# A decoder layer's last microseconds: three PSUM banks for the last down products, one residual moved, sixteen unread products added

## What is computed

```
x = x + q * scan(kv, sigmoid(a))            # gated linear recurrence over the 1024 rows
x = x + layernorm(softmax(q k^T) v Wout)    # 16 heads, 64 context rows and one null key
x = x + bitlinear(silu(bitlinear(n, w_gate)) * bitlinear(n, w_up), w_down)   # hidden width 1024
bitlinear(a, w): a rounded to 8-bit integers by its row's largest value, w rounded to -1, 0, 1
```

## Time and profile before

| what | value |
|---|---|
| median of 3 runs | 516.19 us (515.22 to 517.26) |
| the profiled execution's own time | 514.18 us |
| its span, from first to last instruction | 512.4 us |
| PE busy | 475.0 us, 93% |
| DVE busy | 421.3 us, 82% |
| ACT busy | 330.5 us, 65% |
| POOL busy | 303.9 us, 59% |
| mean granted TensorE clock | 0.992 |

### The profile page before, as it was taken

How to read it: one execution, slowest core, us unless ns; L and a number is a source line. 1 busy time by engine, 2 the same in 40 slices (tenths; PEclk the granted TensorE clock), 3 DMA queues, 4 the chain that set the end, 5 groups by cost and what they waited for, 6 DMA issues and landing times.

```text
span 512.4 us, 8915 instructions
## 1 busy us (share of the span) xinstructions
PE 475.0 (93%) x2962; PEld 389.2 (76%) x2962; DVE 421.3 (82%) x938; ACT 330.5 (65%) x456; POOL 303.9 (59%) x481
## 2 busy tenths in 40 slices
PE   1999999989988998999999999999999999999775
PEld 0777787867767887888888888888888888886433
DVE  5799998958427667899989899898998998987784
ACT  4545541345323434788888889788888888786651
POOL 2223224610001577798788797877878878888860
PEclk9999999999999999999999999999999999999996
DMA  8996000230000000011131211223232122121243
GB/s 262 324 353 252 2 1 1 56 68 0 1 1 1 0 3 6 6 27 42 36 58 37 53 36 43 53 52 38 47 47 47 43 38 56 42 48 42 62 105 91
DMA packets 67116, 31.80 MB, mean 62 GB/s; under 512 B 49664, under 2 KB 65280, under 8 KB 67072
## 3 DMA queue, kind: packets, MB, share of 16 engines
q1 hardware_dynamic: 67072, 31.24, 24.4%
HBM read 15.24 MB, written 4.19 MB: 38 GB/s over the span
## 4 chain that ended last, share of the span: by engine, by line
PE 67%; DVE 17%; POOL 4%; issue 4%; DMA 3%; SPq 3%; ACT 2%; DVEq 0%; POOLq 0%; ACTq 0%
PE psum L1252 34%; PE psum L1505 10%; PE psum L1510 9%; PE psum L1268 3%; DMA xs<-in_x_dram 3%; DVE region_a L940 2%; PE psum L1483 2%; PE psum L1491 2%; PE psum L1386 2%; SPq L394 2%; PE psum L1356 2%; PE psum L1373 1%; DVE region_d L1057 1%; DVE mx L1054 1%; DVE region_a L951 1%
## 5 line engine op out<-in xcount | busy, mean ns | idle before, releaser
L547 POOL TENSOR_TENSOR region_d<-region_d,rden 128x1024 f32<-128x1024 f32 x32 | 60.9, 1904 | 86.9 <-DVE rden L1071 86.9
L1252 PE MATMUL psum<-Mhi,xT2hi 128*128 128x260 f32 x256 | 75.0, 293 | 0.2
L1252 PE MATMUL psum<-Mlo,xT2hi 128*128 128x260 f32 x256 | 72.3, 283 | 0.0
L1252 PE MATMUL psum<-Mhi,xT2lo 128*128 128x260 f32 x256 | 72.3, 283 | 0.0
L1505 PE MATMUL psum<-VW,region_d 128*128 128x256 f32 x256 | 61.1, 381 | 4.8 <-DVE pTn L1156 4.8
L1510 PE MATMUL psum<-VW,region_d 128*128 128x256 f32 x256 | 60.5, 379 | 0.0
L1505 PEld LDWEIGHTS psum<-VW,region_d 128*128 128x128 f32 x256 | 48.1, 190 | 14.8 <-DVE pTn L1156 6.3
L1054 DVE TENSOR_REDUCE mx<-psum 128x8 f32<-128x520 f32 x64 | 44.6, 697 | 11.8 <-PE psum L1252 10.3
L1510 PEld LDWEIGHTS psum<-VW,region_d 128*128 128x128 f32 x256 | 48.6, 190 | 6.6
L1079 DVE SCALAR_TENSOR_TENSOR region_c<-psum,zw,region_c 128x1024 f32<-128x1024 f32 x32 | 41.1, 1283 | 13.3 <-ACT region_c L754 11.7
L1252 PEld LDWEIGHTS psum<-Mhi,xT2hi 128*128 128x128 f32 x256 | 48.2, 188 | 1.3 <-issue 1.0
(11 more groups left out here) (149 smaller groups left out, 1211.4 us busy)
## 6 DMA issues: line engine op xcount, KB each, us to landing
out_dram<-xs SPq DMA_DIRECT2D x32, 128.0 KB, 1.9
xs<-in_x_dram SPq DMA_DIRECT2D x1, 2560.0 KB, 13.3
VW<-in_L_xattn_Wkv_dram SPq DMA_DIRECT2D x1, 2048.0 KB, 12.5
region_b<-in_L_xattn_Wkv_dram SPq DMA_DIRECT2D x1, 2048.0 KB, 17.3
xs<-in_x_dram SPq DMA_DIRECT2D x3, 512.0 KB, 7.0
region_w<-in_L_ffn_w_gate_dram SPq DMA_DIRECT2D x2, 512.0 KB, 9.9
region_w<-in_L_ffn_w_up_dram SPq DMA_DIRECT2D x2, 512.0 KB, 7.8
region_w<-in_L_ffn_w_down_dram SPq DMA_DIRECT2D x8, 128.0 KB, 5.5
```

The source lines that it names most:

```text
L547: pool.tensor_tensor(p2[:, v, 0:H * MK].rearrange("p (h j) -> p h j", j=MK), e[:, :, 0:MK], rden[:, v, :].unsqueeze(2).broadcast_to([P, H, ...
L1252: mm = pe.matmul(dst, lhsT, rhs, start=i == 0, stop=i == len(terms) - 1)
```

## The change

The last three down products go to three banks: down(T-3) to bank 7, down(T-2) to bank 5 as before, down(T-1) to bank 0. So down(T-3) no longer waits for residual(T-4), and down(T-1) no longer for residual(T-2). `residual` takes the bank as an argument. On VectorE residual(T-4) moves from its place ahead of `last_max(T - 1)` to behind the last quantisation, and residual(T-3) from there to behind the copy of the last tile's second half. On TensorE sixteen products of the identity matrix with w_down (256 columns each) are put between down(T-3) and the transposes of the last tile; they write bank 0, and nothing reads them.

```diff
--- before.py
+++ after.py
@@ -1131,11 +1131,11 @@
                 dve.reciprocal(qr[:, v, 0:1], qs[:, v, 0:1]).then_inc(qrh_done, 1)
                 hidden_weight(t + 5, v)
 
-            def residual(n):
+            def residual(n, home=5):
 
                 dve.wait_ge(hw_done, n + 1)
                 dve.wait_ge(down_psum, n + 1)
-                dve.scalar_tensor_tensor(out=xs[:, n, :], in0=bank(5, D), scalar=hw[:, n % 4:n % 4 + 1],
+                dve.scalar_tensor_tensor(out=xs[:, n, :], in0=bank(home, D), scalar=hw[:, n % 4:n % 4 + 1],
                                          in1=xs[:, n, :], op0=ALU.mult, op1=ALU.add) \
                     .then_inc(x3_done, 1)
 
@@ -1225,7 +1225,6 @@
             residual(T - 5)
             scale_h(T - 2)
             last_values(T - 1)
-            residual(T - 4)
             last_max(T - 1)
             scale_h(T - 1)
 
@@ -1235,13 +1234,14 @@
             dve.wait_ge(last_scaled, 1)
             dve.wait_ge(nhT_ready[(T - 1) % 2], 16 * ((T - 1) // 2))
             dve.tensor_scalar(nh_of(T - 1), row, 1.0, -MAGIC, ALU.mult, ALU.add).then_inc(last_quantised, 1)
-            residual(T - 3)
+            residual(T - 4)
             dve.wait_ge(last_psum, 2)
             dve.wait_ge(down_psum, T - 2)
             dve.tensor_copy(nhT3[(T - 1) % 2][:, FC // 2:FC, :].rearrange("p k n -> p (k n)"),
                             bank(6).bitcast(BF16)[:, FI // 2:FI]).then_inc(last_T, 1)
+            residual(T - 3, 7)
             residual(T - 2)
-            residual(T - 1)
+            residual(T - 1, 0)
 
 
         @block.tensor
@@ -1526,7 +1526,14 @@
             down(T - 5, T)
             gate_up(T + 4, (T - 1) % 2)
             down(T - 4, T)
-            down(T - 3, T)
+
+            pe.wait_ge(nhT_ready[(T - 3) % 2], 16 * ((T - 3) // 2 + 1))
+            pe.wait_ge(y2_ready, T)
+            group(bank(7, D), [(nhT3[(T - 3) % 2][:, k, :], wdT[:, k, :]) for k in range(FC)]).then_inc(down_psum, 1)
+
+            pe.wait_ge(silu_ready, T)
+            for k in range(2 * FC):
+                pe.matmul(bank(0, D), ident16[:, :], wdT[:, k % FC, :], start=True, stop=True)
 
             pe.wait_ge(last_quantised, 1)
             pe.wait_ge(pT0_ready, T)
@@ -1535,10 +1542,11 @@
                     mm = pe.transpose(bank(4 + 2 * half_).bitcast(BF16)[:, k * P:(k + 1) * P],
                                       nh_of(T - 1)[:, k * P:(k + 1) * P], ident16[:, :])
                 mm.then_inc(last_psum, 1)
-            down(T - 2, T)
+            pe.wait_ge(nhT_ready[(T - 2) % 2], 16 * ((T - 2) // 2 + 1))
+            pe.wait_ge(x3_done, T - 3)
+            group(bank(5, D), [(nhT3[(T - 2) % 2][:, k, :], wdT[:, k, :]) for k in range(FC)]).then_inc(down_psum, 1)
             pe.wait_ge(last_T, 2)
-            pe.wait_ge(x3_done, T - 1)
-            group(bank(5, D), [(nhT3[(T - 1) % 2][:, k, :], wdT[:, k, :]) for k in range(FC)]).then_inc(down_psum, 1)
+            group(bank(0, D), [(nhT3[(T - 1) % 2][:, k, :], wdT[:, k, :]) for k in range(FC)]).then_inc(down_psum, 1)
 
 
 # ---- launch: one core; inputs and outputs as the reference has them ----
```

## The result

| | before | changed |
|---|---|---|
| median of 19 runs each | 515.51 us (512.66 to 517.26) | 517.71 us (515.66 to 519.45) |
| ratio, 95% interval | | 1.0047 (1.0029 to 1.0064) |
| the profiled execution's time, its span | 514.18, 512.4 us | 517.28, 515.5 us |
| mean granted TensorE clock | 0.992 | 0.993 |

The change makes the kernel slower by 0.47% of 515.5 us, which is 2.4 us, with an interval from 1.5 to 3.3 (the two medians lie 2.2 apart; the ratio is the one on record). The forecast was 2.0 us slower, by half clock in the last two groups.

A forecast was written before the change was run, and what follows sets the result against it. It took the tail's waits as the bound, with T-2's transposing DMA deciding: +2.93 us (DMA) - 0.91 (pause gone) makes residual(T-1) 2.02 later, so a median of 518.2 us, 0.4% slower, range 515.8 to 519.3.

The forecast's parts named there:

- half clock: Last two down groups: TensorE at 1.2 GHz, residual(T-1) 2.02 us later; the forecast's own case, chance 0.55.
- What decides: Tail: T-2's transposing DMA on SP's queue has only 0.3 us of slack ahead of down(T-2).
- The gain of VectorE: VectorE's last quantisation: last_max follows the last hidden layer directly, gaining 0.27 us, off the path.
- SP: SP's queue: store(T-4) waits for the moved residual, so the transposing DMA behind it goes out 3.11 us later.
- the late landing: Rival, transposing DMA of T-2: landing takes 4.3 us, adding 1.3, giving 519.5 us; chance 0.13.
- The delay of down(T-2): TensorE's tail: down(T-2) starts at 508.05 instead of 505.12, a loss of 2.93 us.
- The banks: Last two down groups: separate banks let them run without a pause, giving back 0.91 us.
- The clock: TensorE's tail: about 3 us of idleness behind the transposes drops the clock to half for both last groups.
- The full clock's price: Rival, last two groups at full clock: residual(T-1) 0.31 us later, 516.5 us; full or mixed clock, chance 0.27.
- Nothing holds the DMA: Rival, SP's queue: DMA issued at 501.80 as before, 2.9 us sooner at full clock, 513.3 us; chance 0.05.
- the pause between the groups: Between the starts of down(T-2) and down(T-1): 2.65 us before, 1.74 expected at half clock.

The follow-up runs named there:

- the pause filled: The change with 24 more unread products between the transposes and down(T-2): 517.39 us, ratio 1.0024 against the kernel before.
- the version with the DMA ahead: The change with the transposing DMA of T-2 issued ahead of store(T-4): 514.16 us, ratio 0.9957 against the kernel before.
- the banks alone: The kernel before with the three banks only, residual(T-4) at its old place, no unread products: 514.41 us, ratio 0.9977.

## Why the prediction was right

- **What decides.** The prediction read the chain and then looked for what lay ready beside it, with a slack of 0.3 us. That was the right place: the transposing DMA is the new releaser, and exchanging one line on SP removes the loss.
- **The gain of VectorE.** last_max was to follow the hidden layer by 0.04 us: it starts at 502.11, behind 500.79 + 1.28 = 502.07. The moved residual was to start 0.61 us behind the second quantising step: 505.14 - 504.54 = 0.60.
- **SP.** The store was to be issued 0.03 us behind the residual and take 0.33: 505.65 behind 505.14 + 0.48 = 505.62, and 0.33. The DMA was to follow 0.06 us later: it was 0.10 (505.98 to 506.08). Its landing was to take 3.0 to 3.1 us: 3.03, so the stores close ahead of it and behind it did not delay it, and the late landing did not come. It came in none of the four traces in which the DMA is held: from its issue to TensorE's start it is 3.08 to 3.10 us in each.
- **The delay of down(T-2).** From the start of the last hidden layer it was 505.12 - 499.66 = 5.46 us before and is 509.16 - 500.79 = 8.37 now: 2.91 later, where 2.93 was worked out.
- **The banks.** The groups were to follow each other after 1.74 us at half clock; it was 1.68 (510.84 - 509.16). The last residual was to come 1.98 behind the last group's start; it was 2.02. The sizes of the two nearly cancel.
- **The clock.** Half clock was expected for both groups and came, in the change and also where the transposes had still run at full clock (the change without products). The full clock's price, 0.31 us over before, was measured as 0.33 with the pause filled. The prediction gave half clock only 0.55, and rightly left the matter open: the traces below show the clock doing different things behind the same pause.
- **The other side.** "Nothing holds the DMA" was priced at 2.9 us gained with full clock, and the version with the DMA ahead has 2.94 in the trace, 2.2 in the times. In the change the store, waiting for the residual of 505.14, held a DMA whose data had been ready since 502.79. That fits the sentence of the Trainium skill's page "DMA: Bandwidth & Descriptors", in its section on the anatomy of one DMA, that the issuing sequencer waits before dispatch; that a wait there holds the entries behind it is what the trace of SP's queue adds.

The total was 0.4 us low against the ratio (2.0 worked out, 2.4 measured), inside the interval from 1.5 to 3.3. In the traces it is +2.91 for the DMA, -0.97 for the pause between the groups (2.65 before, 1.68 now) and +0.04 for the last group's end: 1.98, where 2.02 was worked out. The absolute 518.2 stood on a median of 516.19 from 3 runs; over 19 runs before has 515.51, so the forecast lies 0.5 us above the measured 517.71. The prediction held that 2.6 us is the least that can be told from no change; 19 runs of each narrowed that to 0.9 to either side. No step failed. The one term that was mis-sized stands in an experiment: the banks alone give more than 0.91 us where the clock comes back in the second group.

## What to carry to other kernels

When an instruction is moved back on one engine, follow its semaphore to every queue that waits for it, and read what stands behind the waiting entry there. A store that nobody needs can hold a DMA on which the whole tail rests, and the cure is to put the urgent entry ahead of the one that is not. A filler that is to keep TensorE's clock up is worth only as much as the last pause behind it allows: 1.55 us with the DMA ahead, nothing with a pause of 3.25 us behind it. Where executions differ by more than the effect, measure the stretch between two fixed instructions in the traces, beside the whole time, and read the granted clock in the stretch, since a trace is one execution.

## What was not expected of the hardware

The clock's fall does not stand at a fixed place. TensorE paused for 1.80 us ahead of the transposes with the DMA ahead and no products, and for 1.67 in the change without products; in the first the transposes took 0.71 us and the fall came during them, in the second 0.61 us, with a granted clock of 1.00 over the whole window from 504 to 508. With the banks alone the clock rose again in the middle of the last group. The fall can come further ahead, too. In the execution of the change without products TensorE ran at half clock from about 488 to 498:

```profile
486.73 1.04 PE L1252 MATMUL psum<-wgT,region_d 128*128 128x512 bf16 x4 [1.92 <-DMA region_d<-region_c]
487.90 1.86 PE L1252 MATMUL psum<-wuT,region_d 128*128 128x512 bf16 x4
...
495.65 1.92 PE L1252 MATMUL psum<-wdT,region_d 128*128 128x256 bf16 x8
497.36 1.39 PE L1252 MATMUL psum<-wuT,region_d 128*128 128x512 bf16 x4
```

The start of the last hidden layer lay between 499.66 and 502.87 us in the ten traces, without a change to the code ahead of it. That scatter of 3.2 us is as large as the largest effect measured against the kernel before, and the clock accounts for about half of it. At 164.5 us all ten traces have a pause of 2.1 us on TensorE. In four of them the clock stayed up behind it, in the other six it fell. The same two places, first in the trace of before and then with the DMA ahead:

```profile
164.51 0.66 PE L1483 MATMUL psum<-ident,region_d 128*128 128x128 f32 x4 [2.08 <-POOL region_d L550]
166.98 1.89 PE L1505 MATMUL psum<-VW,region_d 128*128 128x256 f32 x8
```

```profile
165.11 0.82 PE L1483 MATMUL psum<-ident,region_d 128*128 128x128 f32 x4 [2.07 <-POOL region_d L550]
169.17 1.89 PE L1505 MATMUL psum<-VW,region_d 128*128 128x256 f32 x8
```

From the one to the other it is 2.47 us in the first and 4.06 in the second, with a granted clock of 1.00 and of 0.68 from 164 to 168. That fall costs 1.6 us. The earliest and the latest start, 3.21 us apart, are those of before and of the banks alone: 1.01 of it is there at the pause, 1.58 come from the fall behind it, and the other 0.62 later. The six traces that have it start their last hidden layer at 501.71 to 502.87. Of the other four, three start it at 499.66 to 500.79, and the fourth, at 502.00, is the one with the half clock from 488. What decides whether the clock falls behind one and the same pause was not found.
